# Reordering one software-pipelined attention step: query turns and the value projection ahead of the scores, the key projection behind them

## What is computed

```python
qkv = x @ Wqkv                       # 128 -> 3 * 1024; 16 heads of 64
q, k = l2norm(q) * qs, l2norm(k) * ksc
q = q * cos * scale + rotate_half(q) * sin * scale      # and k with 1/scale
# windows of 32 queries; each sees its own and the previous 32 keys
attn = softmax(where(mask, -max, q @ k.T * 8))
x = x + (attn @ v) @ Wo
# feed-forward: layernorm, W1 (128 -> 2*341), a * gelu(gate), W2
x = x + ffn(x)
```

## Time and profile before

| | |
|---|---|
| median of 3 runs | 6443.03 us |
| profiled execution: time, span | 6452.24 us, 6450.4 us |
| busy over the span: PE, PE weight loads | 88%, 61% |
| busy: DVE, POOL, ACT | 71%, 66%, 53% |
| mean granted TensorE clock | 0.957 of 2.4 GHz |
| first to last row maximum of each stack | 914.9 to 2688.5 us and 4621.0 to 6396.2 us |

### The profile page before, as it was taken

How to read it: one execution, slowest core, us unless ns; L and a number is a source line. 1 busy time by engine, 2 the same in 40 slices (tenths; PEclk the granted TensorE clock), 3 DMA queues, 4 the chain that set the end, 5 groups by cost and what they waited for, 6 DMA issues and landing times. The chain is left out here.

```text
span 6450.4 us, 186611 instructions
## 1 busy us (share of the span) xinstructions
PE 5702.0 (88%) x76063; PEld 3949.3 (61%) x76063; DVE 4573.9 (71%) x6115; ACT 3401.8 (53%) x4021; POOL 4282.0 (66%) x2122
## 2 busy tenths in 40 slices
PE   7888968888888888889999999999688888888887
PEld 4444447666666666665555555554476666666665
DVE  6455459888888888776556555552588888888886
ACT  1444546666666666523444444434366666666664
POOL 1000058887878888526777777779688878888884
PEclk7898989999999999989999999999799999999999
DMA  0000012222222222100000000000122222222221
GB/s 25 1 1 1 2 52 63 73 61 68 67 65 67 69 60 68 49 9 1 1 1 1 1 1 1 1 1 1 52 61 75 60 74 63 72 67 68 61 68 48
DMA packets 188334, 254.69 MB, mean 39 GB/s; under 512 B 60828, under 2 KB 81816, under 8 KB 187288
## 3 DMA queue, kind: packets, MB, share of 16 engines
q1 hardware_dynamic: 187416, 242.03, 14.4%
HBM read 38.98 MB, written 1.57 MB: 6 GB/s over the span
## 5 line engine op out<-in xcount | busy, mean ns | idle before, releaser
L2094 POOL TENSOR_TENSOR XB<-XB,Pb 128x1024 f32<-128x1024 f32 x448 | 1070.4, 2389 | 338.2 <-ACT Pb L2054 297.3
L908 POOL TENSOR_TENSOR sin_qk<-raw_qk,rot 128x512 f32<-128x512 f32 x768 | 998.2, 1321 | 90.5 <-ACT raw_qk L816 59.6
L2104 DVE TENSOR_REDUCE b_pmax<-slot 128x1 f32<-128x512 f32 x1024 | 653.4, 683 | 324.9 <-PE slot L1841 323.7
L2054 ACT ACTIVATE Pb<-slot 128x1024 f32<-128x1024 f32 x512 | 502.6, 1024 | 702.1 <-PE slot L1952 649.3
L924 POOL TENSOR_TENSOR rot_out<-rot_out,sin_qk 128x1024 f32<-128x1024 f32 x192 | 604.5, 3148 | 401.3 <-DVE rot_out L982 400.3
L941 POOL TENSOR_TENSOR inv_norm<-norm2c,minus_half 128x16 f32<-128x16 f32 x192 | 668.9, 3484 | 167.8 <-DVE norm2c L1083 167.4
L530 PE MATMUL slot<-w_hi,x_hi 128*128 128x512 f32 x1152 | 547.2, 475 | 70.4 <-POOL w_lo L899 46.0
L781 ACT ACTIVATE qT<-slot 128x1024 f32<-128x1024 f32 x192 | 197.1, 1027 | 751.3 <-PE slot L537 751.3
L937 POOL TENSOR_TENSOR inv_norm<-norm2c,minus_half 128x16 f32<-128x16 f32 x192 | 559.3, 2913 | 0.0
L982 DVE TENSOR_TENSOR rot_out<-slot,rot 128x1024 f32<-128x1024 f32 x384 | 468.9, 1221 | 94.5 <-PE slot L537 52.0
L706 PE MATMUL slot<-kT,qT 64*32 64x64 f32 x24576 | 332.0, 229 | 196.2 <-issue 195.8
(11 more groups left out here) (213 smaller groups left out, 13265.8 us busy)
## 6 DMA issues: line engine op xcount, KB each, us to landing
VW<-V SPq DMA_DIRECT2D x1152, 128.0 KB
VW<-V SPq DMA_DIRECT2D x768, 64.0 KB
w_raw<-in_Wqkv SPq DMA_DIRECT2D x36, 512.0 KB, 3.7
Wo<-in_Wo SPq DMA_DIRECT2D x12, 512.0 KB, 4.2
W<-in_W SPq DMA_DIRECT2D x12, 341.0 KB, 3.1
consts<-in_shape_constants SPq DMA_DIRECT2D x1, 2436.5 KB, 9.0
QH<-rows_dram SPq DMA_DIRECT2D x128, 2.0 KB
QB<-rows_dram SPq DMA_DIRECT2D x128, 2.0 KB
```

The costliest lines, as they stand in the source:

```text
L908: ins = pool.tensor_tensor(dst[:, :, x, :], src[:, :, 1 - x, :], tab, ALU.mult)
L2054: act.activation(Pb[:, at % B_RING, :], slot[n % 2][:, :], ACT.Exp).then_inc(s["b_exp"], 1)
L2094: pool.tensor_tensor(b_sum[:, window % 2, :], Pb[:, (at - 1) % B_RING, :] if k == 1 else b_sum[:, window % 2, :], Pb[:, at % B_RING, :], A ...
L2104: dve.tensor_reduce(b_pmax[:, n // 2, u:u + 1], o[:, 512 * x:512 * x + 512], AX.X, ALU.max)\
```

## The change

In the step of the stack, on four engines:
- TensorE: turning the queries and projecting the values (chunk k-1) go ahead of the scores (chunk k-2). The key projection (chunk k) goes ahead of the turn of the outputs. The second value tile of the feed-forward goes ahead of the query projection.
- ScalarE: the raw keys are copied ahead of `OT`. `qT` has two buffers, so its copy waits for the scores of two chunks ago and not of the last one.
- GpSimd: the power for the queries goes ahead of the sine half of the keys.
- VectorE: the cosine half of the queries goes ahead of the row maximum; normalising the queries goes ahead of adding the keys' sine half; the output scaling follows at once, and the feed-forward result, the low part of x and the tables come behind it.
- The two buffers of squares become one.

Nothing is added or removed but buffers. The diff, cut to its core:

```diff
-        sq = [sb(f"sq{i}", [128, INNER], F32, mem) for i in range(2)]
+        sq = sb("sq", [128, INNER], F32, mem)
-        qT = sb("qT", [128, 8, 128], F32, mem)
+        qT = [sb(f"qT{i}", [128, 8, 128], F32, mem) for i in range(2)]
```

TensorE, after probabilities times values (`pv_mm`):

```diff
+                c = at.chunk(1)
+                if c is not None:
+                    pe.wait_ge(s["qn_done"], START + g + c + 1)
+                    wait_for_slot2()
+                    turn(slot[2], rot_out[0]).then_inc(s["tq_mm"], 1)
+                c = at.chunk(1)
+                if c is not None:
+                    if c == 0:
+                        pe.wait_ge(s["w_lo_done"], START + third_of(call, layer, 3))
+                    pe.wait_ge(s["on_done"], START + upto(k - 3))
+                    project_in(slot[1], c % 4, 2).then_inc(s["v_mm"], 1)
```

The same two entries are taken out behind the scores, and the key projection moves from behind the turn of the outputs to ahead of it:

```diff
-                                           qT[r:r + 64, h // 2, 32 * w:32 * w + 32],
+                                           qT[c % 2][r:r + 64, h // 2, 32 * w:32 * w + 32],
...
+                c = at.chunk(0)
+                if c is not None:
...
+                    pe.wait_ge(s["q_copy"], START + g + c + 1)
+                    pe.wait_ge(s["aq_done"], START + g + c + 1)
+                    project_in(slot[0], c % 4, 1).then_inc(s["k_mm"], 1)
```

ScalarE:

```diff
-                    act.wait_ge(s["cq_done"], START + g + c)
-                    act.activation(sq[0][:, :], raw[0], ACT.Square).then_inc(s["q_evac"], 1)
+                    act.wait_ge(s["ck_done"], START + g + c)
+                    act.activation(sq[:, :], raw[0], ACT.Square).then_inc(s["q_evac"], 1)
-                    act.wait_ge(s["s_mm"], START + g + c)
+                    act.wait_ge(s["s_mm"], START + (max(g + c - 1, 0) if isinstance(g, int) else g + c - 1))
-                    act.wait_ge(s["ck_done"], START + g + c)
-                    act.activation(sq[1][:, :], raw[1], ACT.Square).then_inc(s["k_evac"], 1)
+                    act.wait_ge(s["cq_done"], START + g + c + 1)
+                    act.activation(sq[:, :], raw[1], ACT.Square).then_inc(s["k_evac"], 1)
```

GpSimd (the same four lines are taken out behind `sin_half`):

```diff
+                    pool.wait_ge(s["nq_done"], START + g + c + 1)
+                    pool.wait_ge(s["qn_done"], START + g + c)
+                    pool.tensor_tensor(inv_norm[0][:, :], norm2c[0][:, :], minus_half[:, 0:H], ALU.pow)\
+                        .then_inc(s["iq_done"], 1)
                     tables_for(layer, c)
                     pool.wait_ge(s["rk_done"], START + g + c)
                     pool.wait_ge(s["k_copy"], START + g + c + 1)
                     sin_half(1, c, "bk_done")
```

More of the change, by code:

```diff
@@ L643, in step @@
                     mm.then_inc(s["w2_mm"], 1)
+                b = at.block(9)
+                if b is not None:
+                    pe.wait_ge(s["xb_done"], START + 2 * upto(k - 4))
+                    if draining:
+                        pe.wait_ge(s["gelu_done"], START + 3 * (f + b + 1))
+                    first_layer(slot[2][0:128, 512:1024], 0, *FFN_TILES[1]).then_inc(s["value_mm"], 1)
                 c = at.chunk(0)
@@ L731, in step @@
                     turn(slot[2], Os).then_inc(s["ot_mm"], 1)
[L733 to L739, removed]
                 c = at.chunk(1)
@@ L803, in step @@
                     act.activation(x_hi[c % 4][:, :], XA[:, c * 128:c * 128 + 128], ACT.Copy).then_inc(s["xh_done"], 1)
+                c = at.chunk(2)
+                if c is not None:
+                    act.wait_ge(s["k_mm"], START + g + c + 1)
+                    act.wait_ge(s["bk_done"], START + g + c)
+                    act.activation(raw[1], slot[0][:, :], ACT.Copy).then_inc(s["k_copy"], 1)
                 c = at.chunk(5)
@@ L810, in step @@
                        .then_inc(s["ot_sb"], 1)
-                c = at.chunk(2)
-                if c is not None:
-                    act.wait_ge(s["k_mm"], START + g + c + 1)
-                    act.wait_ge(s["bk_done"], START + g + c)
-                    act.activation(raw[1], slot[0][:, :], ACT.Copy).then_inc(s["k_copy"], 1)
                 c = at.chunk(4)
@@ L1008, in step @@
                     cos_half(0, c, "aq_done")
+                c = at.chunk(4)
+                if c is not None:
+                    dve.wait_ge(s["s_mm"], START + g + c + 1)
+                    dve.tensor_reduce(row_max[:, :], slot[3][:, :].rearrange("p (h k) -> p h k", h=H),
+                                      AX.X, ALU.max).then_inc(s["max_done"], 1)
                 c = at.chunk(3)
@@ L1063, in step @@
                                           slot[2][p, 512:640], ALU.add).then_inc(s["xb_done"], 1)
+                b = at.block(9)
+                if b is not None:
+                    hide(layer, f, b, 0)
                 b = at.block(7)
@@ L1083, in step @@
                     dve.tensor_scalar(norm2c[1][:, :], norm2[1][:, :], 1e-24, None, ALU.max).then_inc(s["nk_done"], 1)
+                b = at.block(10)
+                if b is not None:
+                    hide(layer, f, b, 2)
+                c = at.chunk(2)
+                if c is not None:
+                    dve.wait_ge(s["rq_done"], START + g + c + 1)
+                    dve.wait_ge(s["iq_done"], START + g + c + 1)
+                    normalise(0, "qn_done")
+                c = at.chunk(2)
@@ new lines, in step @@
+                b = at.block(11)
+                if b is not None:
+                    if b % NB == 0:
+                        dve.wait_ge(s["b2_in"], START + 16 * (layer + DEPTH * call + b // NB + 1))
+                    dve.wait_ge(s["w2_mm"], START + f + b + 1)
+                    t0 = (b % NB) * 512
+                    for p, o in ((slice(0, 64), 0), (slice(64, 128), 1)):
+                        cols = slice(t0 + o, t0 + o + 512)
+                        dve.scalar_tensor_tensor(out=XA[p, cols], in0=slot[3][p, 512:1024], scalar=ffn_cols[p, 2:3],
+                                                 in1=XB[p, cols], op0=ALU.add, op1=ALU.add).then_inc(s["f_done"], 1)
```

91 lines of the change are left out of this document (23 added, 68 removed).

## The result

| | before | after |
|---|---|---|
| median | 6441.69 us (4 runs, 6433.59 to 6445.8) | 6603.28 us (4 runs, 6596.22 to 6608.87) |
| profiled execution: time, span | 6452.24, 6450.4 us | 6608.87, 6607.1 us |
| mean granted TensorE clock | 0.957 | 0.959 |

The ratio is 1.0257, with an interval of 1.0241 to 1.0273: the change makes the kernel slower by 162 us, where 6364 us was forecast and 6490 was the upper end. The clock is the same, so it has no part in it.

The account below looks back on a forecast made before the run. The new step was taken as bound by a loop, DVE 13.96 us plus TensorE 4.11; with 0.2 for the clamp and 0.15 for uneven steps, 18.42 us against 18.83, saving 79 us: 6364 us, range 6250 to 6490.

Parts of the forecast that it names:

- The stall before the scores: TensorE's wait before the scores, taken for missing instruction packets: slow work placed ahead takes 0.9 us a step off TensorE.
- TensorE's term of the loop: TensorE from value projection to the end of the scores, one part of the shortest possible step: 4.11 us.
- DVE's term: DVE from row maximum to output scaling, the other part of the shortest possible step: 13.96 us.
- Tables and the feed-forward result leave it: In DVE's chain from maximum to output scaling, these entries no longer count toward its 13.96 us.
- The keys' clamp: DVE's clamp beside GpSimd's sine half of the keys: a collision in about one step of four, 0.2 us a step.
- The rest costs nothing: GpSimd's list, one buffer of squares, two of `qT` and V's earlier DMAs add no time.
- The slower one: Rival: stalls add in full to the new loop of 18.07 us; 19.3 us a step, 6529 us, chance 0.21.
- TensorE's gain counts in full: Rival: DVE gets ahead, output scaling is rarely late; 1.0 us a step or more saved, 6250 us, chance 0.13.
- the stall only moves: Rival: packets come at their own rate, the stall moves to values product or key projection; 6443 us, chance 0.14.

Follow-up runs that it names:

- experiment 9: Value projection put back behind the scores, query turn left ahead: on the changed kernel 1.0146; on the version with key normalisation before the maximum and GpSimd tables 0.9901.
- experiment 8: The kernel before the change with only the rotation tables moved to GpSimd, behind its add: 6441.48 us, ratio 0.9973.
- experiment 1: The changed kernel with one entry of VectorE's list moved, the key normalisation ahead of the row maximum: 6408.66 us, ratio 0.9937.
- experiment 2: The changed kernel with GpSimd's add of the queries' sine half cut from 1024 to 16 columns, all orders kept: 6458.48 us, ratio 1.0024.
- Experiment 6: The changed kernel with key normalisation ahead of the maximum, plus tables made three steps later and their scales loaded one chunk later: 6358.99 us, ratio 0.9874.
- experiment 3: The changed kernel with TensorE's order of before (scores ahead of query turn and value projection, key projection last): 6883.25 us, ratio 1.0667.
- experiment 4: The kernel before with query turn and value projection ahead of the scores, two `qT` buffers, one of squares, rest old order: 7047.79 us, ratio 1.0949.

## Why the prediction was wrong, step by step

- **The stall before the scores** was right in place and nearly in size: forecast 0.9 us off each step, measured (95.5 - 13.9) / 91 = 0.90. That missing instruction packets cause it is not shown: the stall answers to slow work ahead of the scores (experiment 9) and not to the tables on DVE (experiment 8), but no run removed the packets.
- **TensorE's term of the loop** was right: 4.11 us forecast. In the step shown, from the end of the output scaling (1534.28) to the maximum (1537.88) it is 3.6; over the 35 steps between 1200 and 2500 us in which DVE does wait for the scores, the mean, worked out from starts and ends, is 4.0, and over all steps there, those that wait on nothing included, 4.13.
- **DVE's term is the step that failed.** Forecast 13.96 us from maximum to output scaling. In the plain step shown it is 1534.28 - 1518.87 = 15.41, where 13.23 was the forecast: 1.36 more in the normalisation (2.58 for 1.22) and 0.89 from the keys' clamp (1.06 for 0.17), together 2.25. Over all steps between 1200 and 2500 us it averages 15.4, 1.4 more than forecast. From the groups of the window that is 0.68 for the two normalisations (2 x (1.555 - 1.215)), 0.38 for the keys' clamp, and 0.42 for waits for TensorE inside the chain (variance 13.8, output scaling 13.8, feed-forward product 5.2, residual 4.5, over 89 steps), which the sum held at nothing because the step that it was added up from had none. 15.39 and 4.13 make 19.53 us, where 13.96 + 4.11 + 0.35 = 18.42 was forecast. The prediction asked, of everything that moves, what waits for what by semaphore; it put a price on DVE's work beside GpSimd only for the clamp, because the earlier trace rows showed one, and said that no row showed a normalisation beside a sine half. But the row that mattered was another: the add in the earlier trace rows with 3.184 us for 1024 columns, where two sine halves of 512 take 2 x 1.321 = 2.64. Its excess is what the two engines already cost each other, and the earlier trace rows show the normalisation right beside it. With the cosine moved ahead of the maximum the change turned round who starts first. Experiments 1 and 2 show it.
- **"Tables and the feed-forward result leave it"** was true of the chain and wrong for the step. What leaves the chain lands behind the output scaling, where only TensorE's 4.1 us cover it: low part of x, four tables, cosine. At the durations of before that is 0.54 + 4 x 0.42 + 1.22 = 3.4 and fits; in the change a table takes 0.895 and x_lo 0.705 on average, and the steps with tables need 4.8 us from the end of the output scaling to the maximum, before which DVE waits 0.06 (means of 17 steps between 1200 and 2500 us, worked out from the trace); the other steps need 3.9. Experiment 6 measured 41 us for it, on the kernel of experiment 1.
- **The keys' clamp** collides as forecast, only more: 0.38 us on average (0.558 - 0.175) for 0.2. The sum also took, without saying so, the queries' clamp at 0.17 us, though it averaged 0.457 before; that came true (0.175).
- **The rest costs nothing**: one buffer of squares, `qT` and V's DMAs show no wait among the largest. The wait of the query turn for the normalised queries (68.5 us) was not in the sum; most of it comes from DVE's late list, since it is 15.7 us in experiment 1 and 23.8 in experiment 2.
- **The rivals.** The slower one had the sign (6529 us at 0.21) but not the mechanism: it wanted 1.0 us of stall left in the loop, and 0.15 are left; the holding was in no rival. That TensorE's gain counts in full fell; so did "the stall only moves".

The sizes add up roughly: 150 us for the holding (experiment 2), 41 for the tables (6), and 0.18 us x 192 = 35 for the clamp, 226 of the 239 us between forecast and result. That they add is an assumption, and 41 was measured on another kernel than the change. With the two repairs the kernel takes 6352.53 us on its chip, 0.9868; the forecast of 6364 us against 6443.03 was 0.9877. That the two agree is luck: it is another kernel, with GpSimd making the tables, and the normalisation ahead of the maximum.

## What to carry to other kernels

When an order is changed, compare not only what each entry waits for but, between VectorE and GpSimd, what runs beside it and which of the two starts first: the later one pays, so let the engine with slack be the later one. Before VectorE work on SBUF operands is moved, look in the trace for a GpSimd or VectorE group whose mean is well above what its size asks for; that excess is a price already being paid, and a reorder can move it to the critical engine. Work that is moved out of a chain needs cover where it lands, at its durations there.

## What the runs showed of the hardware

- **VectorE's normalisation and GpSimd's add, each with all operands in SBUF, do not overlap; the one that starts later is held.** The normalisation takes 1.22 us alone and 2.58 behind the add; the add takes 2.38 alone and 3.20 to 3.21 behind the normalisation. Behind the sine halves it is the same: the low part of x takes 0.28 us beside a power and up to 1.37 beside a sine half, a table 0.41 and up to 1.54. The Trainium skill (SBUF — State Buffer, on the shared port pair) calls the port an exclusive lock between such instructions; these rows agree. In the prediction I drew that rule over the sine halves, and not over the add.
- **With one operand in PSUM nothing is held.** Before, the output scaling, which reads slot 1, ran beside a sine half 44 times in the window, at 1.22 us each; the maximum (1.22 in every kernel) is not held beside the add either.
- **GpSimd's power doesn't hold VectorE, but VectorE holds the power.** In the step shown after the change, the power (L941) runs from 1530.90 to 1534.62, and DVE's normalisation at 1530.65, its add of the keys' sine half at 1531.79 and its low part of x at 1534.20 take 1.21, 1.24 and 0.28 us, their times alone; in 21 other steps a normalisation starts in the middle of a power and takes 1.21 to 1.22. The power itself takes 3.72 to 3.86 us in the 68 steps in which it starts during a normalisation, and 2.90 in the other 21. So the lock above is not held for the whole of a power; when it is held inside one is not shown.
- **A clamp of 128x16 can cost as much as an instruction on 128x1024**: 0.17 us alone, 1.06 in that step beside a sine half, 1.14 on average in experiment 4, all of it waiting. In the change, 76 clamps of the keys run beside a sine half, and each ends 0.03 to 0.14 us after it.
- **The stall between two dense groups of small matmuls answers to slow work put between them**, 95.5, 40.4 and 13.9 us per window for 0, 0.85 and 2.3 us of it. It also shrinks where TensorE waits for other reasons: with nothing between the groups it is 66.0 us in experiment 3, whose mask waits 56.2 us for DVE. Its cost depends on what waits behind the scores: in experiment 4 it was down to 6.4 us and the kernel was 9.5% slower.
